# Two conditioned blocks on one core: GpSimd's weight splits, low bytes and the first recurrence step put in other places

## The reference, cut to what matters

```python
# layer 0, condition: per batch a scaled, normalised weight; x is 16 x 128 x 128
w = scale * weight * y;  w = w * rsqrt(sum(w * w) + 1e-8);  c = einsum('boi,bil->bol', w, x)
# layer 0, feed-forward 128 -> 384 -> 128; each act_qdq needs max|.| over the whole tensor
c = act_qdq(c); up = act_qdq(c @ qdq(w_up).T); gate = act_qdq(c @ qdq(w_gate).T)
g2 = act_qdq(gate * u16(sigmoid(gate)));  o = act_qdq(g2 * up)
x = x + o @ qdq(w_down).T
# layer 1, condition: 128 recurrence steps
h_t = tanh(x_t @ Wx + b + h_{t-1} @ Wh)
# layer 1, 8 experts of 512 hidden units, the best 2 of 8 mixed per token
h1 = gelu(h @ w1[e].T + b1[e]);  y_e = h1 @ w2[e].T + b2[e]
out = x + sum over the top 2 of softmax(router) * y_e
```

## Time and profile before

| | us |
|---|---|
| median of 3 runs | 319.94 (319.29 to 320.16) |
| the profiled execution | 319.01 |
| its span | 317.0 |
| TensorE busy | 258.8 (82%) |
| VectorE busy | 271.3 (86%) |
| ScalarE busy | 212.7 (67%) |
| GpSimd busy | 85.6 (27%) |

### The profile page before, as it was taken

How to read it: one execution, slowest core, us unless ns; L and a number is a source line. 1 busy time by engine, 2 the same in 40 slices (tenths; PEclk the granted TensorE clock), 3 DMA queues, 4 the chain that set the end, 5 groups by cost and what they waited for, 6 DMA issues and landing times.

```text
span 317.0 us, 8438 instructions
## 1 busy us (share of the span) xinstructions
PE 258.8 (82%) x2611; PEld 191.8 (61%) x2611; DVE 271.3 (86%) x648; ACT 212.7 (67%) x432; POOL 85.6 (27%) x158
## 2 busy tenths in 40 slices
PE   5759840010769989999999999999999999999994
PEld 4624340000245677778877777777777777787873
DVE  4889899989897898769999889788789978889885
ACT  6368899544052677777676676776766676688882
POOL 2687999000007822011221210311210211101000
PEclk9979976555698999999999999999999999999999
DMA  6992553100001420000000000000000100001001
GB/s 190 326 272 52 100 100 66 33 0 0 0 0 35 92 44 0 0 3 0 20 0 2 0 2 25 4 0 0 0 2 11 27 0 0 0 1 36 0 2 27
DMA packets 28122, 11.67 MB, mean 37 GB/s; under 512 B 17449, under 2 KB 27074, under 8 KB 28098
## 3 DMA queue, kind: packets, MB, share of 16 engines
q1 hardware_dynamic: 27698, 11.16, 14.7%
q10 hardware_dynamic: 400, 0.20, 0.2%
HBM read 6.11 MB, written 1.05 MB: 23 GB/s over the span
## 4 chain that ended last, share of the span: by engine, by line
PE 71%; DVE 21%; issue 2%; DMA 2%; ACT 1%; SPq 1%; POOL 0%; ACTq 0%; DVEq 0%
PE bank L841 71%; DVE peak L588 5%; DVE big L684 3%; DVE big L694 2%; DMA wn<-in_w_up 2%; DVE big L667 2%; DVE peak L662 2%; DVE big L700 1%; DVE big L702 1%; SPq L263 1%; DVE q L656 0%; DVE wyT L775 0%; DVE big L820 0%; DVE c L631 0%; DVE pkm L581 0%
## 5 line engine op out<-in xcount | busy, mean ns | idle before, releaser
L549 ACT ACTIVATE big<-bank,miscT 128x384 f32<-128x384 f32 (+2 forms) x160 | 96.2, 602 | 31.8 <-PE bank L841 28.5
L841 PEld LDWEIGHTS bank<-wt,big 128*128 128x128 f16 x1536 | 97.2, 98 | 29.1 <-issue 4.3
L841 PE MATMUL bank<-wt,big 128*128 (+1 forms) x1536 | 113.0, 219 | 1.7 <-DVE big L820 0.7
L820 DVE TENSOR_TENSOR big<-big 128x384 f16<-128x384 f32 (+2 forms) x160 | 94.5, 592 | 19.9 <-ACT big L551 15.6
L841 PE MATMUL bank<-big,wt 128*128 128x384 f16 (+2 forms) x480 | 108.8, 335 | 0.2 <-POOL big L374 0.2
L841 PEld LDWEIGHTS bank<-big,wt 128*128 (+1 forms) x480 | 45.8, 115 | 12.3 <-POOL big L374 0.3
L372 POOL CAST big<-q 128x64 f16<-128x64 f32 x32 | 13.4, 420 | 132.8 <-ACT q L539 132.6
L816 DVE CAST big<-big 128x512 f16<-128x512 f32 (+2 forms) x112 | 42.4, 379 | 7.5 <-ACT big L549 5.2
L841 PE MATMUL bank<-q,wxh 128*128 (+1 forms) x254 | 44.9, 252 | 2.1 <-ACT q L511 1.6
L539 ACT ACTIVATE q<-bank,miscT (+1 forms) x112 | 30.6, 274 | 23.0 <-PE bank L841 21.6
L841 PEld LDWEIGHTS bank<-q,wxh 128*128 128x128 f32 x254 | 39.2, 193 | 7.7 <-ACT q L511 3.8
(11 more groups left out here) (146 smaller groups left out, 289.8 us busy)
## 6 DMA issues: line engine op xcount, KB each, us to landing
wnat<-in_w SPq DMA_DIRECT2D x8, 512.0 KB, 7.3
x_sb<-in_x SPq DMA_DIRECT2D x4, 256.0 KB, 4.5
out_block<-wyT SPq DMA_DIRECT2D x16, 64.0 KB
wn<-in_w_gate ACTq DMA_DIRECT2D x1, 192.0 KB, 5.3
wn<-in_w_up SPq DMA_DIRECT2D x1, 192.0 KB, 6.1
wn<-in_w_down SPq DMA_DIRECT2D x1, 192.0 KB, 6.1
b_in<-in_b SPq DMA_DIRECT2D x12, 4.0 KB
wt<-wyT SPq DMA_TRANSPOSE x8, 3.0
```

The costliest lines, as they stand in the source:

```text
L549: A(g32[:, f, 0:w], ps_h[f][:, 0:w], ACT.Gelu, bias=bias, scale=1 / WS).then_inc(g32_done, 1)
L820: V.tensor_tensor(g_lo[:, par, f, 0:w], g32[:, f, 0:w], g_hi[:, par, f, 0:w], ALU.subtract).then_inc(g_lo_done, 1)
L841: return nc.tensor.matmul(o, l, r, start=start, stop=stop, skip_group_check=True)
```

## The change

Nothing that is computed changes. The order and the engines do:

- GpSimd: the splits of pieces 0 and 1 no longer stand ahead of `scale_weights(2)`; pieces 0 to 7 follow it in a row. Pieces 8 to 15 stand behind the split of the first 16 states and a wait for the whole residual (`x1_lo_done` at 5), ahead of `split_b2`. ScalarE and VectorE split none. Pieces 8 to 15 get buffers of their own in `up2`.
- Low bytes of chunks 3 and 4 are taken by GpSimd; VectorE takes none.
- First recurrence step: issued directly behind the input part. Steps 14 and 15 both ahead of the third group of transposes.
- VectorE: `weight_scales(0)` and `(1)` stand behind peaks and inside `peak_to_scale`; `weight_lo(0)` behind it.
- TensorE: `transpose_weights(0)` stands behind all transposes of `c`. The waits for expert weights are one for each expert, in the first chunk, whose loop over expert pairs is written out on TensorE. The waits for the residual, for the copies to `acc` and for `x1_lo_done` are narrowed.

```diff
-W_POOL = 14
+W_EARLY = 8
+LOW_SCALAR = 3
...
+        nat_up = [up2.bitcast(F16)[:, TOK * i:TOK * (i + 2)].rearrange("p (a n) -> p a n", a=4) for i in (2, 4)]
...
-            return (nat_wy if i % 8 < 4 else nat)[:, i % 4, :]
+            return (nat_wy, nat, nat_up[0], nat_up[1])[i // 4][:, i % 4, :]
...
             for i in range(W_CHUNKS):
-                if i < W_POOL:
-                    sp.wait_ge(nat_done, i + 1)
-                else:
-                    sp.wait_ge(w_lo_v, i - W_POOL + 1)
-                sp.dma_start_transpose(wt[:, i, :, :], nat_of(i)).then_inc(wt_t[i // 4], 16)
+                sp.wait_ge(nat_done, i + 1)
+                sp.dma_start_transpose(wt[:, i, :, :], nat_of(i)).then_inc(wt_t[i // 2], 16)
...
-            pool.wait_ge(c_mm, NK)
-            split_weights(0, 2)
             scale_weights(2)
...
-            split_weights(2, 11)
-
-            pool.wait_ge(oq, CH)
-            split_weights(11, W_POOL)
-
+            pool.wait_ge(c_mm, NK)
+            split_weights(0, W_EARLY)
+
+            def low_byte(c):
+
+                pool.wait_ge(oq, c + 1)
+                G.tensor_copy(chunk_of(o_lo, c), chunk_of(up2.bitcast(U8)[:, 0::4], c)).then_inc(o_lo_p, 1)
+                pool.wait_ge(o_lo_p, c + 1 - LOW_SCALAR)
+
+            for c in range(LOW_SCALAR, CH):
+                low_byte(c)
...
             for i in range(done):
                 split_states(i)
+            pool.wait_ge(x1_lo_done, CH)
+            split_weights(W_EARLY, W_CHUNKS)
             split_b2()
...
-            for i in range(W_POOL, W_CHUNKS):
-                weight_hi(i)
...
-            for c in range(CH - 1):
+            for c in range(LOW_SCALAR):
                 low_byte(c)
...
+            scale_c(1)
+            peak_c(0)
+            peak_c(1)
             weight_scales(0)
-            weight_scales(1)
-            peak_c(0)
-            scale_c(1)
-            peak_c(1)
             scale_c(3)
             peak_c(2)
             peak_c(3)
-            peak_to_scale(0, NK, lambda u: link(V.memset(u, 1.0)), lambda: weight_lo(0))
+            peak_to_scale(0, NK, lambda u: link(V.memset(u, 1.0)), lambda: weight_scales(1))
+            weight_lo(0)
...
-            V.tensor_copy(chunk_of(o_lo, CH - 1), chunk_of(up2.bitcast(U8)[:, 0::4], CH - 1)).then_inc(o_lo_v, 1)
             make_x1(CH - 2)
             make_x1(CH - 1)
-            for i in range(W_POOL, W_CHUNKS):
-                dve.wait_ge(w_hi_s, i - W_POOL + 1)
-                V.scalar_tensor_tensor(nat_of(i)[:, FF:2 * FF], wnat[:, i % 2, i // 2, :], WS, nat_of(i)[:, 0:FF], ALU.mult,
-                                       ALU.subtract).then_inc(w_lo_v, 1)
...
                     input_part(0, FIRST_STEPS)
+                    first_step(0)
...
-                    if c >= 2:
+                    if c >= 2 and c + p > 2:
                         first_step((c - 2) * 4 + p)
...
-                first_step(EARLY_STEPS + k)
-                pe.wait_ge(x1_done, CH if k == NK - 1 else CH - 1)
+                if k < 2:
+                    first_step(EARLY_STEPS + k)
+                if k == 2:
+                    for r in range(FIRST_STEPS - 2, FIRST_STEPS):
+                        first_step(r)
+                pe.wait_ge(x1_done, k + 2)
...
+                    if c == 0 and s % NF == 0:
+                        pe.wait_ge(wt_t[e2 * 2 + s // NF], 32)
+                    if c == 0 and first and s in (2, 3, 4):
+                        pe.wait_ge(added, s - 1)
...
-                    if c == 0 and first and s == 2 * NF - 1:
-                        for p in range(1, 4):
-                            pe.wait_ge(wt_t[p], 64)
...
-            pe.wait_ge(x1_lo_done, CH)
+            pe.wait_ge(x1_lo_done, 2)
             input_part(FIRST_STEPS, RNN_FROM[1])
-            pe.wait_ge(added, NK)
-            pe.wait_ge(wt_t[0], 64)
-            chunks(pe, pair)
+            chunks(pe, pair, True)
```

More of the change, by code:

```diff
@@ L138, in program @@
         ld_w = [sem(f"ld_w{i}") for i in range(4)]
-        wt_t = [sem(f"wt_t{i}") for i in range(4)]
+        wt_t = [sem(f"wt_t{e}") for e in range(E)]
         consts, cond_T, cond_sb, norm_in, norm_mm, norm_sb, root_done, norm_done = sems(
@@ L218, in program, with chunks, is_last @@
         o_lo = gate2.bitcast(F16)[:, NJ * TOK:2 * NJ * TOK]
-        def chunks(eng, pair):
+        def chunks(eng, pair, first_unrolled=False):
             for c in range(CH):
                 pair(c, 0, c > 0)
-                with eng.Fori(1, E // 2 - (c == CH - 1)) as e2:
-                    pair(c, e2, True)
+                if c == 0 and first_unrolled:
+                    for e2 in range(1, E // 2):
+                        pair(c, e2, True)
+                else:
+                    with eng.Fori(1, E // 2 - (c == CH - 1)) as e2:
+                        pair(c, e2, True)
             pair(CH - 1, E // 2 - 1, True)
+        def is_last(c, e2):
+            return c == CH - 1 and isinstance(e2, int) and e2 == E // 2 - 1
         def is_first(e2):
@@ L544, in pair @@
                         take_gates(c - 1)
-                    if isinstance(e2, int) and not first and s == 3:
+                    if is_last(c, e2) and s == 3:
                         take_gates(c)
@@ L803, in pair @@
                         add_b2(c - 1)
-                    if isinstance(e2, int) and not first and s == 6:
+                    if is_last(c, e2) and s == 6:
                         add_b2(c, 2)
@@ L886, in _ @@
                 last.then_inc(cT_mm, 1)
-                if k == 1:
-                    transpose_weights(0)
+            transpose_weights(0)
             spread_peak(0)
@@ L954, in _ @@
                     if p == 2:
-                        pe.wait_ge(*((o_lo_done, c + 1) if c < CH - 1 else (o_lo_v, 1)))
-                    if c >= 2:
+                        pe.wait_ge(*((o_lo_done, c + 1) if c < LOW_SCALAR else (o_lo_p, c + 1 - LOW_SCALAR)))
+                    if c >= 2 and c + p > 2:
                         first_step((c - 2) * 4 + p)
```

22 lines of the change are left out of this document (8 added, 14 removed).

## The result

| | before | after |
|---|---|---|
| median | 319.62 (318.50 to 320.16) | 323.27 (322.96 to 323.50) |
| the profiled execution | 319.01 | 323.22 |
| its span | 317.0 | 321.1 |
| start of layer 0's last quantisation (VectorE) | 85.78 | 84.98 |
| recurrence step 1 | 94.64 | 91.93 |

The account below looks back on a forecast made before the run. TensorE and VectorE, both over 80% busy, were taken to bound the kernel (chain 71% and 21%). 319.0 - 0.8 - 0.7 - 3.8 - 0.4 + 10.5 = 323.8, or +4.8 on a median of 319.9: 324.7 us, range 316.5 to 330.

Parts of the forecast that it names:

- Part 1: At the start, moving the splits of pieces 0 and 1 from beside L654 and L656 gains 0.8 us (-0.5 to 1.8).
- Part 2: In the sigmoid stage, GpSimd's splits end sooner and touch fewer VectorE rounds: gain 0.7 us (0 to 1.7).
- Part 3: From 92 to 109.6 us, the recurrence starts earlier, with the clock kept up: gain 3.8 us.
- Writing the loop out: In the experts' first chunk on TensorE, it saves the 0.29 us pause at three loop turns: gain 0.4 us.
- Part 4: In the experts' first chunk, GpSimd's late splits take port turns with VectorE: loss 10.5 us (1 to 16).
- Rival 1: In the experts' first chunk, GpSimd's splits fit beside VectorE: faster, 317.2 us with a loss of 3; chance 0.27.
- rival 2: In the experts' first chunk, the clock falls; ten slots add some 0.3 us each: 327.7 us, chance 0.10.
- rival 3: GpSimd's low byte takes 3 us or more, or the clock falls in 94 to 98: 326.5 us, chance 0.11.
- Rival 4: The recurrence still starts late and the late splits are hidden: 318.4 us, 0.5% faster; chance 0.07.

Follow-up runs that it names:

- 8-column run: The changed kernel with the late splits (pieces 8 to 15) cut to 8 of 512 columns, instructions and waits kept: 312.03 us, ratio 0.977.
- late step 0: The changed kernel with the first recurrence step back behind the wait for chunk 2's high byte: 323.18 us.
- spare matmuls: The changed kernel with six spare 256-column matmuls ahead of each TensorE wait for VectorE in slots 5 to 11 of the first chunk: 323.01 us, ratio 1.0135.
- fills: The 8-column run with 24 GpSimd memsets of 128x512 f32, which write and don't read, in place of the late splits: 313.42 us, ratio 0.980.

## Why the prediction was right, step by step

**Part 1, forecast 0.8: 0.44 by the two traces, and not resolved.** The second group's gate matmuls came at 19.55 in place of 20.39, which is 0.84. The gate peaks came 0.44 sooner (36.89 against 37.33). With 1.0 us between the traces of one start, the part can be anything from nothing to 0.9. I had given the new order of scales and peaks a price of zero on balance; its experiment says that it costs some tenths. I had named the tail of `scale_weights(1)` as able to hold one instruction up, and put it at nothing: it ran into the first L663 (L656 of before), at 1.20 us, so that marker (below 1 us) missed.

**Part 2, forecast 0.7: 0.36 by the same traces** (the last quantisation starts 0.80 sooner, less the 0.44). The two parts together, 0.80 where I had 1.5, are better known than each: after and the kernels of the 8 columns, the late step 0, the spare matmuls and the fills all start the experts between 104.69 and 105.11. The marker held: from the third round on both lines ran undisturbed, and the early splits ended at 48.8 in place of 55.7. The excess that was left stood in the first two rounds, 0.35 and 0.99 us on L674:

```profile
L674 DVE TENSOR_SCALAR big<-big x6: 693/694/1676, 43.2 to 61.6; 128x1024 f32<-128x1024 f32 x6
```

**Part 3, forecast 3.8: 3.87** (109.62 - 104.95 = 4.67, less the 0.80 by which the quantisation started sooner). One half of the gain is shown by the run with the low byte back on ScalarE: it undoes 1.95 of it, the earlier start of step 1. The other 1.9 lie between step 1 and the experts (14.98 us before, 13.02 in after). Steps 1 to 4, the three intervals that I had reckoned with, took 2.49 us (91.93 to 94.42) in place of 4.10, so 1.6 of it comes while the clock is 1.00 in place of 0.69 and 0.50. Why the clock stays up is not shown: it stayed up in the run with the low byte on ScalarE as well. The early first step is 0.1 of the whole at most. The low byte on GpSimd took 2.25 and 1.67 us, and VectorE's instruction beside each:

```profile
92.18 2.25 POOL L370 CAST big<-big 128x1536 f16<-128x1536 uint8 x1 [43.42 <-DVE big L707]
96.10 1.67 POOL L370 CAST big<-big 128x1152 f16<-128x1152 uint8 x1 [1.67 <-DVE big L707]
```

```profile
92.15 0.96 DVE L709 TENSOR_SCALAR big<-big 128x1536 f16<-128x1536 int8 x1
96.00 0.76 DVE L709 TENSOR_SCALAR big<-big 128x1152 f16<-128x1152 int8 x1
```

The 2.25 us are above the 1.5 to 1.9 I bounded it by, but inside its cover of 3.8 us: TensorE waited for neither. And they are not all work. L709 began first each time; the casts ended 1.32 and 1.01 us behind its end. With chunk 3's low byte on ScalarE the last cast began 0.07 us earlier in L709's time, took 1.73 us in place of 1.67, and ended 1.00 us behind L709 again. So here it was VectorE that held GpSimd up, as L702 of before held L326 at 96.48 (1.18 us in place of 0.62). For L702 I had it the other way round; L712 (L719 in after) was held as I had it, 0.72 us where one of its kind takes 0.36.

**Writing the loop out, forecast 0.4: 2.85.** This is the mis-sized term of the sum. I read the pause of 0.29 at the turn as the whole price, and did not compare a slot in the loop with one ahead of it, where each slot with a recurrence step would have shown its 0.17 too.

**Part 4, forecast 10.5: 11.2**, by the 8-column run. Against the same form of loop (27.4 to 27.8 us) the chunk is 11.0 to 11.3 longer. That the cause is GpSimd's instructions taking turns with VectorE's is shown by three runs: shorter ones, a third of them under reductions with the rest on ScalarE, and fills that hold the cast alone. L822's durations came as forecast (0.7 to 1.5), with a median of 0.81 us and 1.34 at most; L818's median was 0.52. TensorE's own waits were 7.1 us on L822 and 0.9 on L777, where I wrote 10. Against the 8-column run, TensorE is idle 6.8 us more in the chunk (8.2 against 1.45) and busy 4.2 us more (30.55 against 26.31), with matmuls at half clock that fill the time VectorE leaves. The splits took from 104.53 to 126.1, 21.6 us, as forecast (22).

```profile
124.89 1.20 POOL L335 TENSOR_TENSOR big<-wnat,big 128x512 f16<-128x512 f32 x1
```

The small instructions of the router, for which I had no row, are held up too. In after:

```profile
116.87 1.12 DVE L760 TENSOR_SCALAR mixd<-mixd 128x2 f32<-128x2 f32 x1
118.09 0.56 DVE L764 TENSOR_TENSOR pick<-pick,mixd 128x16 f32<-128x16 f32 x2
118.69 0.58 DVE L768 TENSOR_TENSOR gates<-pick 128x16 f32<-128x16 f32 x1
```

and the first and the last of them before:

```profile
116.42 0.16 DVE L758 TENSOR_SCALAR mixd<-mixd 128x2 f32<-128x2 f32 x1
116.98 0.17 DVE L766 TENSOR_TENSOR gates<-pick 128x16 f32<-128x16 f32 x1
```

L746 (0.56 in place of 0.15) and the two of L753 (0.66 in place of 0.26) do the same, so the five lines take 2.5 us more. Of the two values that I gave for part 4, 12 us with this and 8.5 without, the measured 11.2 is nearer to the first.

**The rivals.** Rival 1 (the splits fit beside VectorE) falls with the chunk's 38.75 us. Of rival 2 the sign came true, the clock fell to 0.50 in 116 to 124, but no price of 3 us can be seen: with half of that fall lifted, the chunk took 38.73 us in place of 38.75. Of rival 3 the low byte's 2.25 us was longer than I had it, but not 3 us. Rival 4 falls with both markers.

**The sum.** -4.67 ahead of the experts, -2.85 for the loop and +11.2 for the splits give +3.7; measured, +3.65. My own -5.3, -0.4 and +10.5 gave +4.8. The forecast of 324.7 was 1.4 us too high. The loop's gain was 2.45 larger than I had it, and the median of before was 0.3 lower in the second set of runs; the front gained 0.6 less than I had it, and part 4 cost 0.7 more. So that the time came within 1.4 us is in part luck: errors of 2.75 and 1.3 us stood against each other. What holds without luck is that the two large terms, part 3 and part 4, came within 0.1 and 0.7 us by the mechanisms named, with the cause of the higher clock in part 3 left open.

## What to carry to other kernels

Background work on GpSimd isn't free because the engine is idle: in these runs an instruction of it that reads held VectorE's next cast or two-input instruction for what was left of its length. So put it where VectorE reduces, and release it there by a semaphore. The same eight pieces cost 11.2 us beside the experts, 4.8 in a row beside the sigmoid and multiply rounds, and nothing under the peaks, where ScalarE had taken over sixteen of their 24 instructions. When one edit has two parts of opposite sign, undo each by itself: the written-out loop was a good change that a bad one hid.

## What was not expected of the hardware

- A hardware loop on TensorE cost far more than its pause here: 0.95 us a turn of eight slots at 256 columns, of which the pause is 0.34, and about 0.26 at 384 columns.
- The turns go both ways: VectorE's L709, one input, held GpSimd's cast of every fourth byte to float16, so that it took 2.25 us for 1536 elements and 1.67 for 1152, of which 1.32 and 1.01 lie behind L709's end.
- An instruction of VectorE on two elements (L760) took 1.12 us behind a GpSimd instruction, where it takes 0.16 alone.
- A pause of 1.78 us with TensorE idle left the granted clock at 1.00; one of 1.55 us at nearly the same place was followed by 0.50 before. And with the clock of 116 to 120 raised from 0.50 to 1.00, the chunk was no shorter (38.73 and 38.75 us): TensorE was waiting anyway.
- GpSimd's fills stretched VectorE's casts (0.29 us alone, up to 0.74) and left subtractions with two inputs at 0.42.
